# A scan in two parts: the next slot's product between 896 and 128 columns of each scan in a state-space mixer

## What is computed

```python
x = x + 0.5 * ffn(layernorm(x))
x = x + mixer(layernorm(x))
x = x + 0.5 * ffn(layernorm(x))

# mixer, the part that matters here
dA  = exp(delta[..., None] * A)                  # b, l, 512, 16
dBu = delta[..., None] * Bm[:, :, None, :] * u[..., None]
def step(h, inp):                                # over the 1024 tokens
    dA_t, dBu_t, c_t = inp
    h = dA_t * h + dBu_t
    return h, einsum('bdn,bn->bd', h, c_t)
y = (scan(step) + u * D_param) * silu(z)
return y @ out_proj_w
```

## Times and profile before

| | |
|---|---|
| three runs | 3138.5, 3139.1, 3139.45 us, median 3139.1 |
| the profiled execution | 3137.2 us, span of its instructions 3135.4 us |
| busy in the span | PE 85%, DVE 85%, POOL 69%, ACT 54% |
| PE's granted clock, mean | 0.894 |
| scan L1404 | 512 x 2285 ns = 1170 us |
| product L1415 | 512 x 1208 ns = 618 us |
| C times the scan, POOL, L1320 | 512 x 2357 ns = 1205 us |
| replicate L1459 | 1024 matmuls, 368 us |

### The profile page before, as it was taken

How to read it: one execution, slowest core, us unless ns; L and a number is a source line. 1 busy time by engine, 2 the same in 40 slices (tenths; PEclk the granted TensorE clock), 3 DMA queues, 4 the chain that set the end, 5 groups by cost and what they waited for, 6 DMA issues and landing times. The chain is left out here.

```text
span 3135.4 us, 31534 instructions
## 1 busy us (share of the span) xinstructions
PE 2657.7 (85%) x10285; PEld 1379.8 (44%) x10285; DVE 2657.3 (85%) x2498; ACT 1692.0 (54%) x2302; POOL 2149.1 (69%) x1283
## 2 busy tenths in 40 slices
PE   2999999967878978978978978978877669999998
PEld 1566657633314414414414414414412215666665
DVE  6788875549999999999999999999999996777775
ACT  3444444446665665666666666656665534444442
POOL 4566664348877877777777777777878864655553
PEclk9999999988978979979978979968976769999999
DMA  3011111037786786786786686776686760101100
GB/s 108 21 47 45 51 57 34 21 90 189 170 198 163 181 196 162 175 200 162 177 198 162 175 200 161 174 190 170 166 198 167 170 165 27 31 31 34 33 28 20
DMA packets 173144, 387.95 MB, mean 124 GB/s; under 512 B 22470, under 2 KB 89990, under 8 KB 172742
## 3 DMA queue, kind: packets, MB, share of 16 engines
q1 hardware_dynamic: 155302, 367.12, 47.1%
q10 hardware_dynamic: 17696, 19.01, 2.0%
HBM read 308.33 MB, written 52.56 MB: 115 GB/s over the span
## 5 line engine op out<-in xcount | busy, mean ns | idle before, releaser
L1320 POOL TENSOR_TENSOR mix_scan<-mix_scan,mix_bc 128x1024 f32<-128x1024 f32 x512 | 1205.2, 2357 | 394.7 <-DVE mix_scan L1404 394.1
L1404 DVE TENSOR_TENSOR_SCAN mix_scan<-mix_decay,ps_all 128x1024 f32<-128x1024 f32 x512 | 1170.2, 2285 | 62.1 <-ACT mix_decay L1360 19.4
L1459 PE MATMUL ps_all<-mix_stack,mix_sel 96*128 96x512 bf16 x1024 | 367.8, 447 | 366.1 <-DVE mix_scan L1404 352.8
L776 PE MATMUL ps_all<-ffn_w_gate_up,ffn_xT 128*128 128x512 f32 (+1 forms) x1536 | 650.6, 560 | 12.2 <-DVE ffn_h L514 9.9
L1415 DVE TENSOR_TENSOR ps_all<-ps_all,mix_bc 128x1024 f32<-128x1024 f32 x512 | 618.3, 1208 | 38.8 <-PE ps_all L1459 38.1
L1360 ACT ACTIVATE mix_decay<-mix_decay,mix_a_neg 128x1024 f32<-128x1024 f32 x512 | 573.7, 1141 | 118.9 <-DMA mix_decay<-delta_rows 117.9
L776 PEld LDWEIGHTS ps_all<-ffn_w_gate_up,ffn_xT 128*128 128x128 f32 x1536 | 277.5, 191 | 242.6 <-issue 198.2
L1459 PEld LDWEIGHTS ps_all<-mix_stack,mix_sel 96*128 96x128 bf16 x1024 | 78.8, 103 | 672.5 <-DVE mix_scan L1404 551.3
L514 DVE TENSOR_TENSOR ffn_h<-ffn_silu_gate,ps_all 128x704 f32<-128x704 f32 x128 | 113.6, 888 | 274.5 <-ACT ffn_silu_gate L697 271.0
L1441 PE MATMUL ps_all<-mix_scan,mix_red 128*32 128x512 f32 x2048 | 339.8, 745 | 4.8 <-POOL mix_scan L1320 4.8
L654 POOL TENSOR_TENSOR ffn_h_scaled<-ffn_h,ffn_h_recip 128x1408 f32<-128x1408 f32 x64 | 168.6, 2635 | 243.4 <-ACT ffn_h_recip L746 243.4
(11 more groups left out here) (137 smaller groups left out, 3692.4 us busy)
## 6 DMA issues: line engine op xcount, KB each, us to landing
mix_decay<-delta_rows SPq DMA_DIRECT2D x512, 512.0 KB, 7.3
mix_stack<-mix_parts SPq DMA_DIRECT2D x384, 64.0 KB, 2.0
delta_rows<-mix_delta SPq DMA_DIRECT2D x32, 512.0 KB, 3.1
ffn_x<-_attn_hidden_states_dram SPq DMA_DIRECT2D x32, 256.0 KB, 3.1
after_ffn<-ffn_y SPq DMA_DIRECT2D x32, 256.0 KB, 3.1
normed_ffn<-ffn_y_normed SPq DMA_DIRECT2D x32, 256.0 KB, 3.2
mix_x_tokens<-normed_ffn SPq DMA_DIRECT2D x32, 256.0 KB, 12.4
mix_x_residual<-after_ffn ACTq DMA_DIRECT2D x32, 256.0 KB, 4.1
```

The costliest lines, as they stand in the source:

```text
L776: ins = M(psG[:, lo:hi], xT[:, j % 2, (t * KX + k) * P:(t * KX + k + 1) * P], wgu[:, k, lo:hi], start=(k == 0), stop=(k == KX - 1))
L1320: G.tensor_tensor(wt, wt, bc[r % 2][:, 1, :], ALU.mult).then_inc(hc_done, 1)
L1404: V.tensor_tensor_scan(w[:, slot % RING, :], da[:, slot % SPREADS, :], ps_du[:, slot % 2, :], 0.0, ALU.mult, ALU.add).then_inc(scan_done, 1)
L1459: ins = M(ps_du[:, slot % 2, h * 512:(h + 1) * 512], const.sel[0:SEL, i, :], stack[:, c % 2, q, h * 512:(h + 1) * 512], start=True, stop=True)
```

## The change

Each scan is made as two instructions, of the columns 0 to 895 and 896 to 1023; the second starts from column 895 of the first's result, read from `w`. On DVE the order is: first part of n, product of n+1, second part of n. `scan_done` counts twice per slot, and all who wait for it wait for twice the number, that is for the second part. PE's replicate is divided: `replicate(n, h)` makes one half and counts `rep_du` by itself. Half 0 of slot n+2 now stands at the end of PE's slot n and waits for the first part of scan n alone; half 1 of slot n+1 stands at the beginning of slot n and waits for both parts of scan n-1. The gate stands ahead of the first part of its slot's scan, which is behind the second part of the slot before.

```diff
--- before.py
+++ after.py
@@ -880,6 +880,7 @@
 STORE_SLOTS = {slot + 1: k for slot, kind, k in JOBS if kind == "O"}
 GATE = 4
 LAST_LOAD_SLOT = 48
+SCAN_CUT = 896
 LEAD = 2
 QUAD = 6
 
@@ -1274,7 +1275,7 @@
                 if s == 0:
                     sy.wait_ge(delta_kept, 16 * chunk(R, c))
                 elif slot >= SPREADS or r > 0:
-                    sy.wait_ge(scan_done, n - SPREADS + (1 if s == SLOTS - 1 else 0))
+                    sy.wait_ge(scan_done, 2 * (n - SPREADS + (1 if s == SLOTS - 1 else 0)))
                 row = c * P + 32 * (s % 4) + 8 * (s // 4)
                 sy.dma_start(da[:, slot % SPREADS, :],
                              delta_dram[r % 2, row:row + NCH, :].unsqueeze(0).to_broadcast([NST, NCH, L]))\
@@ -1315,7 +1316,7 @@
                 for slot in slots(r):
                     c, s = divmod(slot, SLOTS)
                     if core(r, full):
-                        pool.wait_ge(scan_done, R * 64 + (slot + 1))
+                        pool.wait_ge(scan_done, 2 * (R * 64 + slot + 1))
                         wt = w[:, slot % RING, :]
                         G.tensor_tensor(wt, wt, bc[r % 2][:, 1, :], ALU.mult).then_inc(hc_done, 1)
                     b, cc = (R, c + 1) if c < 3 else (R + 1, 0)
@@ -1395,30 +1396,46 @@
                 dve.wait_ge(taken["Z"], chunk(b, c) * 2)
                 V.tensor_tensor(u[b % 2][:, c, :], ps_y[:, :], zs[:, c % 2, :], ALU.mult).then_inc(yg_done, 1)
 
-            def scan(r, R, slot):
-                n = R * 64 + (slot + 1)
-                dve.wait_ge(exp_done, n)
-                dve.wait_ge(dbu_done, n)
-                if slot >= 8 or r > 0:
-                    dve.wait_ge(y_made, R * 16 + (slot - 8) // 4 + 1)
-                V.tensor_tensor_scan(w[:, slot % RING, :], da[:, slot % SPREADS, :], ps_du[:, slot % 2, :], 0.0,
-                                     ALU.mult, ALU.add).then_inc(scan_done, 1)
+
+
+
+            def times_b(n):
+                R, slot = divmod(n, 64)
+                dve.wait_ge(rep_du, 2 * (n + 1))
+                if slot == 0:
+                    dve.wait_ge(taken["B"], (R + 1) * 4)
+                V.tensor_tensor(ps_du[:, slot % 2, :], ps_du[:, slot % 2, :], bc[R % 2][:, 0, :], ALU.mult)\
+                 .then_inc(dbu_done, 1)
+
+            def scan(n, part):
+                R, slot = divmod(n, 64)
+                cols = slice(0, SCAN_CUT) if part == 0 else slice(SCAN_CUT, L)
+                if part == 0:
+                    dve.wait_ge(exp_done, n + 1)
+                    dve.wait_ge(dbu_done, n + 1)
+                    if n >= 8:
+                        dve.wait_ge(y_made, R * 16 + (slot - 8) // 4 + 1)
+                    start = 0.0
+                else:
+                    dve.wait_ge(scan_done, 2 * n + 1)
+                    start = w[:, slot % RING, SCAN_CUT - 1:SCAN_CUT]
+                V.tensor_tensor_scan(w[:, slot % RING, cols], da[:, slot % SPREADS, cols], ps_du[:, slot % 2, cols],
+                                     start, ALU.mult, ALU.add).then_inc(scan_done, 1)
 
             def program(r, R, full):
                 for slot in slots(r):
                     c, s = divmod(slot, SLOTS)
-                    if core(r, full):
-                        n = R * 64 + (slot + 1)
-                        dve.wait_ge(rep_du, n)
-                        if slot == 0:
-                            dve.wait_ge(taken["B"], (R + 1) * 4)
-                        V.tensor_tensor(ps_du[:, slot % 2, :], ps_du[:, slot % 2, :], bc[r % 2][:, 0, :], ALU.mult)\
-                         .then_inc(dbu_done, 1)
-
-                    if s == GATE and (c > 0 or r >= 1) and core(r, full):
+                    if not core(r, full):
+                        continue
+                    n = R * 64 + slot
+                    if n == 0:
+                        times_b(0)
+                    if s == GATE and (c > 0 or r >= 1):
                         gate(*((R, c - 1) if c > 0 else (R - 1, 3)))
-                    if core(r, full):
-                        scan(r, R, slot)
+                    scan(n, 0)
+                    if n + 1 < B * 64:
+                        times_b(n + 1)
+                    scan(n, 1)
             rounds(dve, program)
             after.vector(dve, FIRST)
             gate(B - 1, CHUNKS - 1)
@@ -1447,27 +1464,29 @@
                 if h == 1:
                     ins.then_inc(y_made, 1)
 
-            def replicate(r, R, slot):
-
+            def replicate(n, h):
+
+                R, slot = divmod(n, 64)
                 c, s = divmod(slot, SLOTS)
                 i, q = divmod(s, 4)
-                if s == 0:
+                if s == 0 and h == 0:
                     pe.wait_ge(stacked[c % 2], 16 * 12 * (R * 2 + (c // 2 + 1)))
-                if slot > 1 or r > 0:
-                    pe.wait_ge(scan_done, R * 64 + (slot - 1))
-                for h in range(2):
-                    ins = M(ps_du[:, slot % 2, h * 512:(h + 1) * 512], const.sel[0:SEL, i, :],
-                            stack[:, c % 2, q, h * 512:(h + 1) * 512], start=True, stop=True)
-                ins.then_inc(rep_du, 1)
+                if n >= 2:
+                    pe.wait_ge(scan_done, 2 * (n - 2) + 1 + h)
+                M(ps_du[:, slot % 2, h * 512:(h + 1) * 512], const.sel[0:SEL, i, :],
+                  stack[:, c % 2, q, h * 512:(h + 1) * 512], start=True, stop=True).then_inc(rep_du, 1)
 
             def program(r, R, full):
                 jobs = job_list(r, full)
                 for slot in slots(r):
                     c, s = divmod(slot, SLOTS)
-                    if slot == 0 and core(r, full):
-                        replicate(r, R, 0)
-                    if slot < 63 and core(r, full):
-                        replicate(r, R, slot + 1)
+                    at = R * 64 + slot
+                    if at == 0:
+                        replicate(0, 0)
+                        replicate(0, 1)
+                        replicate(1, 0)
+                    if core(r, full) and at + 1 < B * 64:
+                        replicate(at + 1, 1)
                     for h in range(2):
                         m, late = divmod(slot - QUAD - h, 4)
                         if late == 0 and m >= 0 and core(r, full):
@@ -1480,6 +1499,8 @@
                                 pk, prel, pn = prev
                                 pe.wait_ge(taken[pk], nth(pk, R + prel, pn))
                             make(pe, r, R, kind, rel, n, bank)
+                    if core(r, full) and at + 2 < B * 64:
+                        replicate(at + 2, 0)
             rounds(pe, program)
             for h in range(2):
                 sum_quad(B - 1, B - 1, 15, h)
```

## The result

The changed kernel takes 3185.2 us (median of four runs, 3183.9 to 3188.3) against 3139.3 (3138.5 to 3140.5): 1.0147 times as long, 95% interval 1.0135 to 1.0160, so 46 us **slower**. The profiled execution took 3184.3 us, its span is 3182.5. The forecast of 3172 was 13 us too low; the measured time lies inside the forecast's range of 3155 to 3188.

The account below looks back on a forecast made before the run. DVE bounds the kernel, PE not far behind. Per batch +9.9 stalls, -6.0 quiet slots, +0.3 gates make +4.2 us, about 33 over 8 batches; 3137.2 + 33 + 1.9 = 3172 us, range 3155 to 3188.

Parts of the forecast that it names:

- Quiet slot: DVE slot without a gate: 3.50 us falls to 3.40, 60 slots giving 6.0 us less per batch.
- A gate slot: DVE in slots 4, 20, 36, 52: 4.53 us against 4.45, +0.3 us per batch.
- The mechanism: PE's replicate may be only 1.44 us late, 1.34 less than before, so DVE stalls: +9.9 us per batch.
- The signs that the prediction named: Quiet slots at 3.40 us, product's wait from 38 to some 90 us, gates waiting in slots 4, 20, 36, lower DVE share.
- slot 20: Slots 20 and 21: stalls of 0.79 us at the product, 0.59 at the gate, 0.88 at scan 21; +1.5 per batch.
- slots 4 and 57: Slot 4: product stall 0.56 us, gate 0.59, +1.1; slot 57: 0.9, part of a +1.5 with slots 49 and 52.
- another stretch at half clock in a heavy place: Clock rival, PE: costs the same 5 us, giving 3200 us; chance 0.02.
- slot 40: Product waiting for PE: stall 0.7 us now, +1.3 us per batch.
- A dear small scan: Rival, DVE: second scan part loses its overlap, 0.09 us more per slot, 5.4 per batch, 3196 us; chance 0.12.
- The dependence was hidden: Rival, DVE, claimed the opposite: product keeps its 1.30 us, slot 3.58, 13.5 per batch, 3247 us; chance 0.04.
- Works as meant: Rival: stalls stay as they are, 46 us won, 3093 us; chance 0.06.
- POOL and SP, costed at 0: They wait for part 1, start 1.2 us later against the product, but keep their distance; cost 0.

Follow-up runs that it names:

- the split alone: The kernel before with only the scan made in two parts of 896 and 128 columns, back to back, old order, replicate undivided: 3241.1 us.
- late release: The kernel before with one wait added on PE, so the replicate of n+1 also waits for the product of n: 3213.3 us.
- the runs with PE's work cut: Both kernels with one convolution tap, one accumulated matmul in P, Z, X, O and no u x D: 3074.5 us old order, 3055.5 new.
- the run with both halves together: The changed kernel with both replicate halves of n+1 at the head of PE's slot n: 3184.8 us.
- the cut at 512: The changed kernel with the scan cut at column 512 instead of 896: 3218.4 us.
- one more filler: The kernel before with the filler of slots 13, 16 and 33, plus two matmuls of constants in empty slot 46: 3131.1 us.
- the filler: Both kernels with transposes in slot 13 made four times, matmuls of D in slots 16 and 33 twice: changed 3144.9 us, before 3113.9.

## Why the prediction was right, step by step

**DVE.** Quiet slot 3.40 forecast, 3.41 measured (1.91 + 1.12 + 0.38 for 1.94 + 1.12 + 0.34): the second part was dearer than taken, by its start value or its wait, and the first cheaper. A gate slot 4.53 and 4.55, as forecast. The wait that is hidden is 0.18 us, as read from the gate row; the split alone shows it directly. The Trainium skill (VectorE: DVE Perf Modes, The DRAIN you can't avoid) says that a semaphore after each operation costs nothing over one at the end. For an instruction that waits on the one right before it the trace disagrees again, 1.30 against 1.12.

**PE.** The mechanism was right, and late release and the runs with PE's work cut show it from both sides. The signs that the prediction named came too: the product's wait at 104 us (some 90 forecast), gates that wait for PE, a lower busy share of DVE. The terms, in us per full batch:

| place | forecast, added | measured, added |
|---|---|---|
| slots 2 to 4 and the gate | 1.1 | 1.5 |
| 16, 17 | 1.5 | 1.1 |
| 19 | 0 | 1.7 |
| 20 to 22 | 1.5 | 1.3 |
| 29 | 1.6 | 1.4 |
| 36 to 38 | 1.4 | 2.6 |
| 40 | 1.3 | 0.4 |
| 49, 53, 57 | 1.5 | 1.7 |
| quiet slots and gate slots | -5.7 | -5.0 |
| sum | +4.2 | +6.7 |

The batches do not all lose the 6.7: from first product to first product, the first lost 3.0 us, the second 5.6, the sixth 3.1 (the old order itself stalled at its slots 52 and 53) and the last 5.5, so that the mixer is 45 us longer in all; the forecast had 33.

At slot 20, worked in full, the product lost 0.80 (0.79 forecast), the gate 0.57 (0.59), the next scan 0.66 (0.88). That the product's term fits is partly luck. The prediction took only one half of the replicate off the time that PE may be late and came to 1.44 us; the half that was moved stands behind the same late jobs, as the run with both halves together shows, and the bound is 1.19. The lateness was forecast at 2.23 us and was 1.97, and the two errors cancel. At slots 4 and 57 they did not: 0.75 and 1.18 of stall at the product instead of 0.56 and 0.9.

Two more terms were mis-sized by the clock: slot 19, and about 1.2 of the 2.5 us at the product of slot 36. The prediction had this as a rival ("another stretch at half clock in a heavy place", 0.02) and named 5 us per batch for it; it was about 3, and came together with the forecast case rather than in its place.

At slot 40 the prediction took 1.3 us off DVE's way to the product, counted from the end of scan 38. But PE's heavy work there does not start from a scan: the output projection in slot 38 waits for ACT's silu of z, and ACT has the exponential of scan 37 shortly before, for which scan 37 waits in both kernels. The projection starts 4.91 us after scan 37 in both. From the start of that scan to the product of slot 40 (first the old order, whose product is the 1546.05 of the earlier trace rows) it is 9.96 and 9.97 us:

```profile
1536.09 2.29 DVE L1404 TENSOR_TENSOR_SCAN mix_scan<-mix_decay,ps_all 128x1024 f32<-128x1024 f32 x1 [0.65 <-ACT mix_decay L1360]
...
1557.71 2.02 DVE L1422 TENSOR_TENSOR_SCAN mix_scan<-mix_decay,ps_all 128x896 f32<-128x896 f32 x1 [0.54 <-ACT mix_decay L1361]
1567.68 1.23 DVE L1407 TENSOR_TENSOR ps_all<-ps_all,mix_bc 128x1024 f32<-128x1024 f32 x1 [1.12 <-PE ps_all L1476]
```

Counted from there DVE would need 9.20 us in the old order and 8.76 in the new, so only 0.44 is added. A wait that ties DVE to PE just ahead of a place takes away most of the 1.3 us. That coupling of places, which I left out, has its part also in the forecast of the cut at 512, which was too high.

**Rivals.** A dear small scan: 0.38 instead of 0.34, so 0.04 of the 0.09 us allowed, made up by the first part. The dependence was hidden. Works as meant: with PE's work cut the change does win, but 19 us, since half clock keeps PE late even then. Counting the places over the bound was the right thing to do; the bound is 1.19 us and not 1.44, and three more places are over it in the changed kernel: slots 2, 19 and 49, of which the prediction had the last as near its bound. POOL and SP, costed at 0, did stay out of it: PE's `sum_quad` waits 4.5 us for POOL over the span (4.8 before), and DVE's wait for exponentials is 17.4 us (19.4).

## What to carry to other kernels

A change that shortens the busiest engine's instructions is to be read for what it does to the order in which that engine frees and asks for buffers: here 0.09 us was won in each of 480 slots, and 1.6 us of the time that the second engine may be late was lost in every slot, which some ten places per batch had needed. Before moving an instruction forward in its queue, list per slot how late its producer starts, and subtract; two rows per slot are enough, where no other wait ties the two engines together shortly before. And a batch of stalls that follows a light slot of PE may be its clock: filling that slot with idle matmuls gave 0.8% in the old order, but the place has to be tried, for one more filler took back 17 of the 25 us.

## What the runs showed of the hardware

- On DVE an instruction that waits for the one right before it starts 0.18 us (behind a product of 1024 columns) or 0.14 us (behind a scan of 896) later than one that doesn't (1.30 against 1.12, 2.05 against 1.91). A scan part of 0.38 us between the two hid it, one of 0.18 us did so but for at most 0.02.
- A second scan part, which reads its start value from a tile and has one satisfied wait, takes 0.07 us more from start to start than a first part that starts from a constant (1.18 against 1.11 at 512 columns); a second part of 128 columns takes 0.38, one of 32 columns 0.18.
- PE's granted clock fell to its lower level in slots that are heavy themselves, after one slot with gaps of 0.42 and 1.11 us in it. In the changed kernel it fell in the same slots in batches 2 to 6. Small shifts of PE's work move these places, and the gap just before does not decide alone: with the filler the same gap of 0.94 us was followed by a fall in batches 1, 3 and 5 and by none in 2, 4 and 6.
